# The last stage of a two-layer kernel in quarters: loads and stores by four tiles, statistics behind the sums tile by tile

## The reference

```python
x = x + _layernorm(_L0_attn_ref(_layernorm(x), ...))     # attention-like block with a linear recurrence and an MLP
x = x + _layernorm(_L0_ffn_ref(_layernorm(x), ...))      # mixture of experts
return x
```

```python
shared = einsum('ts,sh->th', silu(x @ sw_gate) * (x @ sw_up), sw_down)
combine = ...                                  # top-2 softmax weights, 0 for the other experts
h = silu(einsum('th,ehi->eti', x, w_gate)) * einsum('th,ehi->eti', x, w_up)
routed = einsum('eth,te->th', einsum('eti,eih->eth', h, w_down), combine)
shared_out = sigmoid(x @ shared_gate_w)[:, None] * shared
return routed + shared_out
```

## Time and profile before

| | us |
|---|---|
| median of 3 runs | 642.36 (641.7 to 642.75) |
| the profiled execution | 641.28 |
| its span in the trace | 639.5 |
| TensorE busy | 536.0 (84%) |
| VectorE busy | 411.9 (64%) |
| ScalarE busy | 258.9 (40%) |
| GpSimd busy | 109.7 (17%) |

### The profile page before, as it was taken

The page is one execution under the profiler, slowest core; times in us unless marked ns, Lnnn a source line. Parts: engine busy times, 40 slices in busy tenths (PEclk is TensorE's granted clock), DMA queues, the critical chain, the costliest instruction groups (busy, mean ns, idle before and its releaser), DMA issues.

```text
span 639.5 us, 8171 instructions
## 1 busy us (share of the span) xinstructions
PE 536.0 (84%) x2464; PEld 425.0 (66%) x2464; DVE 411.9 (64%) x1249; ACT 258.9 (40%) x463; POOL 109.7 (17%) x133
## 2 busy tenths in 40 slices
PE   2835358999469999999989998999879799999690
PEld 1423335587347687887677886888667699999580
DVE  6886653789873898974687872417646366766136
ACT  3711344433445414456424335111641256666103
POOL 1600002200002232002204000040001334444200
PEclk9977679999768999999989997999969989999996
DMA  8961000000010002010001000010050324443523
GB/s 303 421 159 33 0 2 0 1 0 34 33 33 1 0 35 67 34 34 33 1 2 66 0 34 33 2 67 20 14 178 28 109 81 127 120 135 102 196 108 131
DMA packets 29485, 44.42 MB, mean 69 GB/s; under 512 B 3147, under 2 KB 24139, under 8 KB 29099
## 3 DMA queue, kind: packets, MB, share of 16 engines
q1 hardware_dynamic: 24451, 32.95, 16.2%
q0 software_dynamic: 3408, 9.38, 3.9%
q10 hardware_dynamic: 1584, 1.57, 0.9%
HBM read 27.55 MB, written 16.34 MB: 69 GB/s over the span
## 4 chain that ended last, share of the span: by engine, by line
PE 54%; DVE 33%; ACT 5%; issue 4%; DMA 2%; POOL 0%; DVEq 0%; POOLq 0%; ACTq 0%; SPq 0%
PE psum L709 10%; PE psum L710 10%; PE psum L711 9%; PE psum L750 8%; PE psum L776 5%; PE psum L719 3%; PE psum L825 3%; PE psum L946 2%; DVE SM L1304 2%; DVE rt L985 2%; DVE rt L984 2%; PE psum L916 1%; PE psum L899 1%; DMA YF<-y_routed 1%; DVE XC L1178 1%
## 5 line engine op out<-in xcount | busy, mean ns | idle before, releaser
L621 ACT ACTIVATE SM<-psum 128x512 f32<-128x512 f32 (+1 forms) x56 | 33.1, 594 | 137.6 <-PE psum L711 103.6
L1304 DVE TENSOR_TENSOR SM<-SM,psum 128x512 f32<-128x512 f32 (+1 forms) x56 | 38.1, 683 | 63.7 <-ACT SM L621 63.5
L497 POOL DMA_INDIRECT x_dispatched<-XN,dest x32 | 32.9, 1027 | 184.7 <-DVE XN L1371 176.2
L750 PE MATMUL psum<-WOU,SM 128*128 128x256 f32 x256 | 60.2, 380 | 0.3 <-DVE SM L1304 0.3
L776 PE MATMUL psum<-WQKV,HT 128*128 128x512 f32 (+1 forms) x128 | 50.7, 549 | 6.8 <-ACT GA L608 3.3
L488 POOL TENSOR_TENSOR OG<-QKV,hvec 128x256 f32<-128x256 f32 x16 | 13.3, 833 | 243.9 <-ACT IG L563 224.9
L750 PEld LDWEIGHTS psum<-WOU,SM 128*128 128x128 f32 x256 | 48.1, 189 | 9.2 <-DVE SM L1304 1.0
L506 POOL DMA_INDIRECT y_routed<-GO,g_dest x39 | 37.7, 968 | 56.8 <-ACT GO L684 56.5
L750 PE MATMUL psum<-SDN,SM 128*128 128x256 f32 (+1 forms) x192 | 44.8, 382 | 2.7 <-DVE SM L1304 2.6
L776 PEld LDWEIGHTS psum<-WQKV,HT 128*128 128x128 f32 x128 | 26.5, 212 | 29.4 <-issue 24.7
L750 PEld LDWEIGHTS psum<-SDN,SM 128*128 128x128 f32 (+1 forms) x192 | 35.8, 189 | 10.2 <-DVE SM L1304 4.1
(11 more groups left out here) (271 smaller groups left out, 1331.0 us busy)
## 6 DMA issues: line engine op xcount, KB each, us to landing
XG<-x_dispatched SPq DMA_DIRECT2D x39, 130.0 KB, 2.5
YF<-y_routed SPq DMA_DIRECT2D x2, 2048.0 KB, 10.9
RUPR<-rup SPq DMA_DIRECT2D x1, 2816.0 KB
X<-x SPq DMA_DIRECT2D x4, 512.0 KB, 6.7
x_after_attention<-X SPq DMA_DIRECT2D x4, 512.0 KB, 2.8
QKV<-x ACTq DMA_DIRECT2D x3, 512.0 KB, 3.5
y_shared<-SH SPq DMA_DIRECT2D x3, 512.0 KB, 2.9
SHF<-y_shared SPq DMA_DIRECT2D x1, 1536.0 KB, 9.6
```

The source lines that it names most:

```text
L497: nc.gpsimd.indirect_dma_start(XD[:, :], bass.IndirectOffsetOnAxis(dest[:, i, old + j:old + j + 1], 0), XN[:, j, :], None).then_inc(dispat ...
L621: nc.scalar.activation(SM[0:rows, g % 3, 0:tb], p_pair(n)[0][0:rows, 0:tb], ACT.Silu).then_inc(silu_ready, 1)
L750: last = nc.tensor.matmul(p_down[:, j // 2, (j % 2) * D:(j % 2 + 1) * D], SM[0:rows, g % 3, j * P:(j + 1) * P], weight[0:rows, m, :], star ...
L1304: nc.vector.tensor_tensor(SM[0:rows, g % 3, 0:tb], SM[0:rows, g % 3, 0:tb], value_rows(n, rows)[:, 0:tb], ALU.mult).then_inc(hid_ready, 1)
```

## The change

Only the last stage is edited. YF is loaded by four DMAs of four tiles each (1 MB), each with a semaphore of its own, and TensorE waits for the quarter that a tile is in. The results are stored by four DMAs of four tiles each (512 KB). VectorE doesn't wait for eight sums before the first `bn_stats`: before that of tile n it waits until n's pair of tiles (its PSUM bank) is summed. For the second half, each `bn_stats` is followed by the final addition of one tile of the first half. Aggregation, square root and ScalarE's work stay in halves of eight.

```diff
+QUARTER = NT // 4
...
+            for i in range(4):
+                q = slice(i * QUARTER, (i + 1) * QUARTER)
+                pairs = YD[2 * q.start * P:2 * q.stop * P, :].rearrange("(j p k) d -> p j (k d)", p=P, k=2)
+                sp.dma_start(YF[:, q, :], pairs).then_inc(yf_in[i], 16)
+            for i in range(4):
+                sp.wait_ge(out_ready, (i + 1) * QUARTER)
+                sp.dma_start(quarter_rows(out, i), x_tiles(i * QUARTER, QUARTER)).then_inc(stored, 16)
+            sp.wait_ge(stored, 16 * 4)
...
-            for g in range(len(FIN)):
-                pe.wait_ge(yf_in[g], 16)
-                for n in range(FSTART[g], FSTART[g + 1]):
-                    for i in range(2):
-                        last = add_to_tile(n, YF[:, n, i * D:(i + 1) * D], start=False, stop=i == 1)
-                    last.then_inc(sum_psum, 1)
+            for n in range(NT):
+                if n % QUARTER == 0:
+                    pe.wait_ge(yf_in[n // QUARTER], 16)
+                for i in range(2):
+                    last = add_to_tile(n, YF[:, n, i * D:(i + 1) * D], start=False, stop=i == 1)
+                last.then_inc(sum_psum, 1)
...
-            def finish(g):
-                for n in range(FSTART[g], FSTART[g + 1]):
-                    dve.wait_ge(fin_normed, n + 1)
-                    x = x_tiles(n, 1)[:, 0, :]
-                    nc.vector.tensor_tensor(x, x, sh_tile(n), ALU.add).then_inc(out_ready, 1)
+            def finish(n):
+                dve.wait_ge(fin_normed, n + 1)
+                x = x_tiles(n, 1)[:, 0, :]
+                nc.vector.tensor_tensor(x, x, sh_tile(n), ALU.add).then_inc(out_ready, 1)
...
-                dve.wait_ge(sum_psum, FSTART[g + 1])
-                stats(nj, lambda j: f_tile(FSTART[g] + j), (fst, fmv, va))
+                for j in range(nj):
+                    dve.wait_ge(sum_psum, (FSTART[g] + j) // 2 * 2 + 2)
+                    step(nc.vector.bn_stats(fst[:, j, :], f_tile(FSTART[g] + j)))
+                    if g > 0 and j < FIN[g - 1]:
+                        finish(FSTART[g - 1] + j)
+                settle()
+                aggregate(nj, (fst, fmv, va))
                 link(rsqrt(r[:, 0:nj], *scratch(nj)))
                 minus_mean(nj, shift, r, fmv).then_inc(fin_stats, 1)
-                if g > 0:
-                    finish(g - 1)
-            finish(len(FIN) - 1)
+            for n in range(FSTART[len(FIN) - 1], NT):
+                finish(n)
```

More of the change, by code:

```diff
@@ L309, in build @@
                   "gdest_ready", "gw_ready"))
-        xf_in, sf_in, yf_in = sem("xf_in"), sem("sf_in"), [sem(f"yf_in{g}") for g in range(len(FIN))]
+        xf_in, sf_in, yf_in = sem("xf_in"), sem("sf_in"), [sem(f"yf_in{i}") for i in range(4)]
         sum_psum, fin_stats, fin_normed = map(sem, ("sum_psum", "fin_stats", "fin_normed"))
@@ L440, in _, with quarter_rows @@
                 sp.wait_ge(go_kept[i], 16 * len(range(i, NG, ORING)))
-            def group_rows(dram, g):
-                return dram[FSTART[g] * P:FSTART[g + 1] * P, :].rearrange("(j p) d -> p j d", p=P)
-            for g in range(len(FIN)):
[L445 to L450, removed]
+            def quarter_rows(dram, i):
+                return dram[i * QUARTER * P:(i + 1) * QUARTER * P, :].rearrange("(j p) d -> p j d", p=P)
+            for i in range(4):
[6 more added lines that the diff above has]
+            sp.wait_ge(stored, 16 * 4)
         @block.gpsimd
@@ L1000, in stats, with aggregate @@
             def stats(nj, tile, own):
+                for j in range(nj):
+                    step(nc.vector.bn_stats(own[0][:, j, :], tile(j)))
+                settle()
+                aggregate(nj, own)
+            def aggregate(nj, own):
                 s, m, a = own
-                for j in range(nj):
-                    step(nc.vector.bn_stats(s[:, j, :], tile(j)))
-                settle()
                 for j in range(nj):
```

## The result

The changed kernel takes 634.13 us in the median of 4 runs (633.31 to 634.61), the one before 642.25 in the median of 4 (641.7 to 642.75): 8.1 us less, a ratio of 0.987 with a 95% interval of 0.9856 to 0.9885. Forecast were 635.3 us and a range of 633.9 to 637.6. The profiled execution took 634.61 us with a span of 632.8; before these were 641.28 and 639.5.

A forecast was written before the change was run, and what follows sets the result against it. The bound was the last stage's chain of YF load, matmuls, statistics, additions and store. Issuing the last store earlier (5.3 us) and landing it faster (1.8) sum to 7.1 us off the median 642.36: 635.3 us, range 633.9 to 637.6.

The forecast's parts named there:

- Part 1: YF loads in quarters: the first lands at 604.8 us instead of the first half's 607.46, the others by 612.8.
- C: Rival on YF loads: quarters come two by two, the first landing no sooner than 607.46; 639.5 us, chance 0.05.
- D: Rival on YF loads: the queue serves all four in turn, landing together at 612.8; slower, 644.8 us, chance 0.04.
- E: Rival on YF loads: first landing in between, at 609 to 611.5 us; no change within 0.2%, chance 0.02.
- Part 2: TensorE idles 1.5 us instead of 4.2, its clock stays full; tile 7 summed at 611.9, tile 15 at 618.8.
- A: Rival on TensorE: the clock falls even in the 1.5 us gap, costing 1.7 us; 637.0 us, chance 0.12.
- Parts 3 and 4: VectorE: statistics follow sums, first aggregation at 612.73; then additions alternate with statistics at 0.334 us, second aggregation at 621.65.
- B: Rival on VectorE: alternating statistics and additions don't overlap, 0.45 us each, +1.6 us; 636.9 us, chance 0.07.
- Part 5: The end: ScalarE paces the last additions, last store issued at 629.18 instead of 634.49, 5.3 us earlier.
- Part 6: Stores in quarters: the last store, 512 KB, lands in 2.8 us instead of 4.6, 1.8 us less.
- The distance to the median: Whole kernel: the 7.1 us span difference was taken off the runs' median of 642.36 us, giving 635.3.

The follow-up runs named there:

- without alternation: Changed kernel with all eight first-half additions moved after the second half's aggregation: 633.94 us, beside 633.34 for the changed kernel and 642.64 for the one before.
- three early additions: Changed kernel with three first-half additions between the second half's statistics and five after its aggregation: 632.53 us, beside 633.34 for the changed kernel.
- the kernel that kept TensorE busy: Kernel before, with ten tiles' shared output written to PSUM twice so TensorE works through the gap: 639.83 us, beside 641.88 for the kernel before.

## Why the prediction was right, point by point

All moments here are from the issue of YF's first load, the predicted ones less 598.99, the measured ones less 599.48.

| step | predicted | measured |
|---|---|---|
| first quarter lands | 5.8 | 5.6 |
| TensorE's gap | 1.5 | 1.42 |
| first aggregation starts | 13.7 | 13.7 |
| first addition between statistics | 17.65 | 17.6 |
| second aggregation starts | 22.7 | 22.6 |
| last store issued | 30.2 | about 30.1 |
| last store's time | 2.8 | 2.8 |
| end of the span | 33.4 | 33.3 |

- **Part 1** held: the queue serves the quarters in order, which was against C, D and E. The first landed after 5.6 us, the last 12.1 us after its own issue, which is 13.6 after the first one's (13.8 predicted). The estimate by the Trainium skill (DMA: Bandwidth & Descriptors, section "Anatomy of one DMA — SWDGE (gpsimd) path"), 4.4 us, was 1.2 too low. The page fits its figures to DMAs that GpSimd issues, and these were issued by SyncE; the measurement decides.
- **Part 2** held: the clock stayed at full through the gap, so A did not come about in this trace, nor in those of the change run again, without alternation and with three early additions, where the gap was 1.42, 1.36 and 1.46 us and the 64 records took 14.08 us each time. That the clock's part is 1.5 us is shown by the kernel that kept TensorE busy; the prediction had put it at 1.7, half of the 3.4 us at the low clock, but TensorE was working in only 2.9 of them. That it would stay up was a choice with one row for it and one against, and no run tried a gap between 1.46 and 4.1 us at this place.
- **Parts 3 and 4** held: the alternation ran at 0.335 us an operation (617.06 to 621.75, fifteen starts), so B is out. That VectorE and not TensorE is late in the second half was shown by taking the alternation out. What the prediction left unsaid is that VectorE's new order, statistics and additions together, brings nothing of the second aggregation's 4.2 us: the loads alone give all of it, since the alternation spends the 2.0 us that the statistics tile by tile save.
- **Part 5** held, with ScalarE setting the pace of the last additions.
- **Part 6** held for the whole change (the last store landed in 2.8 us), but its 1.8 us aren't the price of the size alone. The 4.6 us of the old last store held some 0.5 us of waiting behind the store ahead, and VectorE's order, which sets the two stores further apart, removes this by itself. So the parts one by one differ from the prediction's terms: alone the stores give 1.5 (1.8 predicted), VectorE's order 1.5 (1.1), the loads 4.3 (4.2). They add up to 7.3, against 7.2 together.

**The distance to the median** is the term that was mis-sized: the medians differ by 8.1 us, the tails by 7.2, so some 0.9 us lie ahead of the last stage, which the edit doesn't touch. The trace of before took 641.28 us, 1.0 below its median, the trace of after 634.61, 0.5 above its own. I took a difference of traces off a median of runs and so predicted 635.3 for 634.13.

Executions of one kernel differ in their mean granted clock, and in part with it in their time. Of 24 runs of the kernel before on one chip, 13 had a mean clock of 0.901 to 0.903 and took 642.72 us in the median (641.77 to 643.3), and 6 had 0.911 to 0.914 and took 641.24 (640.88 to 641.77). The 5 in between, 0.904 to 0.908, took 641.34, so above 0.903 the time doesn't follow the clock any more. The changed kernel's 8 runs all had 0.911 to 0.917 and took 633.05 to 634.61, 633.5 in the median: 7.7 us less than the 6 runs with a like clock. So it is likely that some of the 8.1 us is a mix of clocks. That isn't shown: no run varies the clock of the earlier stages by itself, and the change raises the mean a little of its own (3.4 us at half speed less are 0.003 of it). Whether the changed kernel meets the lower clock as often in more runs is open: eight are few, and the kernel with three early additions had 0.906 in 2 of 5.

That 634.13 lies in the stated range is luck in part. The forecast's own range was said to start at 634.0, but the terms given for it, 0.2 us for the earlier landing and 0.5 for the scatter, lead from 635.3 to 634.6, and its upper end to 636.4 instead of 636.2. The mechanism of the last stage was right step by step; the part of the gain that lies ahead of it was not forecast.

## What to carry to other kernels

When a stage is a chain of load, sum, statistics and store, splitting the first load and the last store pays by the bytes that the first and the last consumer don't need, and the clock of TensorE can pay once more when the gap ahead of it becomes short. Work that fills an engine's idle time is free only as long as that engine isn't itself late: give it as many pieces as fit before the next thing that others wait for, and the rest afterwards. Price a transfer from one of the same buffer that had no transfer just ahead of it, and price a change against several runs where executions differ in their clock.

## What was not expected of the hardware

- VectorE's `tensor_scalar` on 128x8 values took 0.59 to 0.65 us instead of 0.17 beside GpSimd's additions of 128x256 (0.72 us each), in both kernels that had them.
- A store's time depended on how far ahead the previous one was: 1 MB from X took 4.6 us behind another issued 2.7 us earlier, and 4.1 when that was 7.4 us ahead; 512 KB took 3.0 to 3.2 us when issued 1.34 us apart and 2.8 to 2.9 when 1.86 us or more apart; the last one of 256 KB took 2.3 us in one kernel and 2.8 in another, where the stores ahead of it were closer together.
- Stores from XF moved at 342 to 348 GB/s, stores from X at 383 to 388, before and after the change; a store of 1 MB from XF took 4.4 to 4.5 us with nothing ahead of it.
- More work on TensorE made the kernel faster: twenty more matmul records in a gap shortened the tail by 1.5 us.
